# A decoder layer with eight experts on one core: new orders of the stages of each step, a router without casts, the last norm in nine batches, an expert's first rows fetched ahead of the next weights

## The reference

```python
x = ln(x + retention(x))          # 16 heads of 16; (q k^T * decay) v + 256 * q past_kv; group norm over the sequence
x = ln(x + cross_attention(x, ctx))  # 16 heads, causal softmax, Wo and bias
x = ln(x + experts(x))            # softmax router over 8 experts, the best two with weights that sum to 1
# an expert: gelu(x @ w_fc[e] + b_fc[e]) @ w_proj[e] + b_proj[e], hidden size 1024
```

## Time and profile before

| | |
|---|---|
| median of 3 runs | 1025.81 us (1024.01 to 1027.06) |
| the profiled execution, own time | 1028.0 us |
| its span in the profile | 1026.2 us |
| busy: TensorE, VectorE, ScalarE, GpSimd | 940.7 (92%), 674.0 (66%), 604.8 (59%), 386.6 (38%) |

### The profile page before, as it was taken

The page is one execution under the profiler, slowest core; times in us unless marked ns, Lnnn a source line. Parts: engine busy times, 40 slices in busy tenths (PEclk is TensorE's granted clock), DMA queues, the critical chain, the costliest instruction groups (busy, mean ns, idle before and its releaser), DMA issues.

```text
span 1026.2 us, 29954 instructions
## 1 busy us (share of the span) xinstructions
PE 940.7 (92%) x10845; PEld 827.9 (81%) x10845; DVE 674.0 (66%) x2054; ACT 604.8 (59%) x1521; POOL 386.6 (38%) x630
## 2 busy tenths in 40 slices
PE   5899999999999999999888998999999999999950
PEld 4788888887887887778777887999999999999950
DVE  3557877877777777787754674575565775575537
ACT  3456566565566665665546475566665675675534
POOL 0224544554455455554443422222232222233223
PEclk7899999999999999999989998999999999999985
DMA  8111131111111111113110434523425432523327
GB/s 271 46 33 53 49 126 64 44 64 55 52 44 54 54 59 48 43 49 110 38 43 27 104 65 121 133 43 55 130 44 139 116 63 42 143 42 46 47 41 317
DMA packets 57075, 79.92 MB, mean 78 GB/s; under 512 B 5696, under 2 KB 46016, under 8 KB 56832
## 3 DMA queue, kind: packets, MB, share of 16 engines
q1 hardware_dynamic: 41216, 58.50, 17.6%
q0 software_dynamic: 13536, 18.16, 10.5%
q10 hardware_dynamic: 2208, 1.73, 0.6%
HBM read 52.10 MB, written 29.71 MB: 80 GB/s over the span
## 4 chain that ended last, share of the span: by engine, by line
PE 53%; DVE 25%; ACT 8%; issue 7%; DMA 2%; POOL 2%; SPq 1%; another core or an unknown queue 0%; ACTq 0%; DVEq 0%; POOLq 0%
PE bank L799 14%; PE bank L813 9%; DVE row_max L1237 7%; PE bank L500 6%; PE bank L815 5%; DVE ret_p L1232 3%; PE bank L587 3%; PE bank L662 2%; PE bank L707 2%; PE bank L582 2%; ACT max_rows L1022 2%; ACT h_f L1131 2%; PE bank L615 2%; PE bank L636 2%; ACT h_parts L1125 2%
## 5 line engine op out<-in xcount | busy, mean ns | idle before, releaser
L799 PE MATMUL bank<-xs_hi,w_both 128*128 128x256 f32 x1152 | 243.9, 289 | 0.0
L1125 ACT ACTIVATE h_parts<-bank,bfc_s 128x256 fp32r<-128x256 f32 x288 | 140.0, 486 | 164.2 <-PE bank L799 158.6
L1679 POOL DMA_INDIRECT residual_sum<-y_w,meta_i x72 | 120.0, 1666 | 306.7 <-DVE y_w L1498 282.8
L1456 DVE TENSOR_TENSOR h_parts<-h_f,h_parts 128x256 fp32r<-128x256 f32 x288 | 121.5, 425 | 152.4 <-ACT h_f L1131 138.9
L813 PE MATMUL bank<-w_both,h_parts 128*128 128x512 f32 x544 | 200.5, 398 | 1.5 <-DVE h_parts L1456 1.5
L799 PEld LDWEIGHTS bank<-xs_hi,w_both 128*128 128x128 f32 x1152 | 193.0, 191 | 8.4 <-issue 2.3
L799 PE MATMUL bank<-xs_lo,w_both 128*128 128x256 f32 x576 | 163.7, 284 | 0.0
L815 PE MATMUL bank<-w_both,h_parts 128*128 128x256 f32 x544 | 153.3, 282 | 0.0
L1131 ACT ACTIVATE h_f<-bank,bfc_s 128x256 f32<-128x256 f32 x288 | 139.3, 484 | 4.4 <-DVE h_parts L1456 3.9
L813 PEld LDWEIGHTS bank<-w_both,h_parts 128*128 128x128 f32 x544 | 102.8, 189 | 20.4 <-DVE h_parts L1456 4.2
L799 PEld LDWEIGHTS bank<-xs_lo,w_both 128*128 128x128 f32 x576 | 110.5, 192 | 0.1
(11 more groups left out here) (185 smaller groups left out, 2161.5 us busy)
## 6 DMA issues: line engine op xcount, KB each, us to landing
rows<-sent_rows SPq DMA_DIRECT2D x37, 258.0 KB
xc_raw<-in_turned SPq DMA_DIRECT2D x32, 256.0 KB, 3.0
w_raw<-in_w_fc SPq DMA_DIRECT2D x8, 1024.0 KB
w_raw<-in_w_proj SPq DMA_DIRECT2D x8, 1024.0 KB
x_t<-in_x SPq DMA_DIRECT2D x32, 128.0 KB, 2.5
residual_sum<-x_row SPq DMA_DIRECT2D x32, 128.0 KB, 1.8
last_in<-residual_sum SPq DMA_DIRECT2D x8, 512.0 KB, 6.6
result<-last_out SPq DMA_DIRECT2D x8, 512.0 KB, 2.7
```

The costliest lines, as they stand in the source:

```text
L799: last = mm(ps_h(g, j), w[:, at:at + P], v[:, k, :], start=(n == 0), stop=(n == 3 * NCH - 1))
L1125: A(h_hi[j % 4][:, :], ps_h(g, j), ACT.Gelu_apprx_tanh, bias=bias)
L1456: V.tensor_tensor(h_lo[j % 4][:, :], h_f[j % 2][:, :], h_hi[j % 4][:, :].bitcast(f32), ALU.subtract).then_inc(s["h_split"], 1)
L1679: G.indirect_dma_start(total, bass.IndirectOffsetOnAxis(meta_i[:, half:half + 1], 0), y_w[:, half, :], None, compute_op=ALU.add)\
```

## The change

All engines get new lists for the steps. TensorE: max_turn(k-1) ends both kinds of step; prep_k and prep_kx stand right behind the scores; max_scores of the even step stands ahead of gn_mean. ScalarE: the four exponentials stand together, ahead of y_out. VectorE: row maxima ahead of ln1_stats in odd steps too; max_split(k-1) ends the even step and precedes pick in the odd. GpSimd: the even step holds shares of k-4 and of k-3, the odd none; in the odd step send stands ahead of gn_rstd. pick compares the integer index itself, put's sum writes integers itself. SP: expert e's first rows, then the weights of e+1 (for e from 1 to 6), then its other rows. The last norm has nine batches (256, seven times 512, 256 rows), and VectorE normalizes a row only in the last one.

For SP, the router and the last norm the diff stands with its minus lines:

```diff
+LAST = (2, 4, 4, 4, 4, 4, 4, 4, 2)
...
-NLAST = N_TOK // (4 * P)
-last_in = [sb(f"last_in{i}", [P, 4, C]) for i in range(NLAST)]
-last_out = [sb(f"last_out{i}", [P, 4, C]) for i in range(NLAST)]
+NLAST = len(LAST)
+last_in = [sb(f"last_in{i}", [P, n, C]) for i, n in enumerate(LAST)]
+last_out = [sb(f"last_out{i}", [P, n, C]) for i, n in enumerate(LAST)]
...
-GN, LN1, LN2, TOP, PUT, SHARE = 3, 3, 3, 4, 4, 4
+GN, LN1, LN2, TOP, PUT, SHARE = 3, 3, 3, 3, 3, 4
...
+def load_rows(e, at, g):
+    sp.wait_ge(s["rows_turned"], g + EVER)
+    sp.wait_ge(s["meta_ready"], g + EVER)
+    apart(sp)
+    sp.dma_start(rows[:, :, :],
+                 sent[ds(e, 1), ds(at, SLOT), :].rearrange("e (h p) c -> p (e h) c", p=P))\
+        .then_inc(s_rows, 16)
     apart(sp)
     for r in range(4):
         sp.wait_ge(s_sent[r], 32 * (B // 4))
-    with sp.Fori(0, n_slots) as j:
-        sp.wait_ge(s["rows_turned"], before + j + EVER)
-        sp.wait_ge(s["meta_ready"], before + j + EVER)
+    load_rows(e, 0, before)
+    if 0 < e < E - 1:
+        sp.wait_ge(s["raw_split"], e + 1)
         apart(sp)
-        sp.dma_start(rows[:, :, :],
-                     sent[ds(e, 1), ds(j * SLOT, SLOT), :].rearrange("e (h p) c -> p (e h) c", p=P))\
-            .then_inc(s_rows, 16)
-    if has_after:
-        sp.wait_ge(s["raw_split"], e + 2)
-        apart(sp)
-        load_weights(e + 2)
+        load_weights(e + 1)
+    with sp.If(n_slots > 1):
+        with sp.Fori(1, n_slots) as j:
+            load_rows(e, j * SLOT, before + j)
 experts(expert, slots)
...
-total_v = total[0:N_TOK, :].rearrange("(b p j) c -> b p j c", p=P, j=4)
-out_v = out.rearrange("b t c -> (b t) c").rearrange("(b p j) c -> b p j c", p=P, j=4)
+def rows_of(rows, b):
+    at = sum(LAST[:b]) * P
+    return rows[at:at + LAST[b] * P, :].rearrange("(p j) c -> p j c", p=P)
+out_rows = out.rearrange("b t c -> (b t) c")
-    sp.dma_start(last_in[b][:, :, :], total_v[b]).then_inc(s_last[b], 16)
+    sp.dma_start(last_in[b][:, :, :], rows_of(total, b)).then_inc(s_last[b], 16)
-    sp.wait_ge(s["last_act"], 3 * (b + 1))
-    sp.wait_ge(s["last_dve"], b + 1)
-    sp.dma_start(out_v[b], last_out[b][:, :, :]).then_inc(s["out_stored"], 16)
+    sp.wait_ge(s["last_act"], sum(LAST[:b + 1]) - (b == NLAST - 1))
+    if b == NLAST - 1:
+        sp.wait_ge(s["last_dve"], 1)
+    sp.dma_start(rows_of(out_rows, b), last_out[b][:, :, :]).then_inc(s["out_stored"], 16)
...
```

```diff
-for j in range(1, 4):
+for j in range(b == NLAST - 1, LAST[b]):
...
-ch.link(V.tensor_copy(top_f[:, :], top_i[:, 0:2]))
-                        top_f[:, :].unsqueeze(2).to_broadcast([P, 2, E]), ALU.is_equal))
+                        top_i[:, 0:2].unsqueeze(2).to_broadcast([P, 2, E]), ALU.is_equal))
-ch.link(V.reduce_sum(pos_f[:, :], place2[:, :, :], AX.X))
-ch.link(V.tensor_copy(pos[c.r][:, :], pos_f[:, :]))
+with nc.allow_low_precision(reason="places are whole numbers, summed in fp32 and written as integers"):
+    ch.link(V.reduce_sum(pos[c.r][:, :], place2[:, :, :], AX.X))
...
-    for j in range(4):
+    for j in range(LAST[b]):
-    for j in range(4):
+    for j in range(LAST[b]):
-    V.tensor_scalar(last_ve[:, b, :], last_mv[:, b, :, 1], EPS, None, ALU.add)\
+    V.tensor_scalar(last_ve[:, b, 0:LAST[b]], last_mv[:, b, 0:LAST[b], 1], EPS, None, ALU.add)\
-    V.scalar_tensor_tensor(out=last_nm[:, b, :], in0=last_mv[:, b, :, 0], scalar=-1.0,
-                           in1=last_rs[:, b, :], op0=ALU.mult, op1=ALU.mult)\
+    V.scalar_tensor_tensor(out=last_nm[:, b, 0:LAST[b]], in0=last_mv[:, b, 0:LAST[b], 0], scalar=-1.0,
+                           in1=last_rs[:, b, 0:LAST[b]], op0=ALU.mult, op1=ALU.mult)\
-    V.tensor_scalar(last_out[b][:, 0, :], last_in[b][:, 0, :], last_mv[:, b, 0, 0:1],
-                    last_rs[:, b, 0:1], ALU.subtract, ALU.mult).then_inc(s["last_dve"], 1)
+    if b == NLAST - 1:
+        V.tensor_scalar(last_out[b][:, 0, :], last_in[b][:, 0, :], last_mv[:, b, 0, 0:1],
+                        last_rs[:, b, 0:1], ALU.subtract, ALU.mult).then_inc(s["last_dve"], 1)
```

Of the step functions the new lists (lines that stay have no plus sign, though they may stand elsewhere in the list); the old ones stand in the code above. TensorE:

```diff
 def step(k):
     odd = k % 2
+    if not odd:
+        run(ret_scores, At(k))
+        run(att_back, At(k - 3))
+        run(x1_turn, At(k - 1))
+        pair_run(prep_kx, k // 2)
+        run(qx, At(k - 1))
+        run(att_proj, At(k - 3))
+        run(att_scores, At(k - 2))
+        run(ret_values, At(k))
+        run(rank, At(k - 4))
+        run(max_scores, At(k - 1))
+        run(gn_mean, At(k))
+        run(y_back, At(k))
+        run(x2_turn, At(k - 3))
+        run(att_values, At(k - 2))
+        run(logits, At(k - 3))
+        run(prep_v, At(k + 1))
+        run(o_turn, At(k - 2))
+        run(max_turn, At(k - 1))
     if odd:
+        run(ret_scores, At(k))
+        run(att_back, At(k - 3))
         pair_run(prep_k, (k + 1) // 2)
+        run(x1_turn, At(k - 1))
+        run(att_proj, At(k - 3))
+        run(qx, At(k - 1))
+        run(att_scores, At(k - 2))
+        run(ret_values, At(k))
+        run(rank, At(k - 4))
         pair_run(prep_q, (k + 1) // 2)
         run(gn_mean, At(k))
+        run(y_back, At(k))
+        run(max_scores, At(k - 1))
         run(x2_turn, At(k - 3))
+        run(att_values, At(k - 2))
+        run(logits, At(k - 3))
+        run(prep_v, At(k + 1))
+        if k < B - 1:
+            run(o_turn, At(k - 2))
             run(max_turn, At(k - 1))
```

ScalarE (its first lines, for k = -1, and its last, for weight splitting, are as before):

```diff
+    if not odd:
+        run(x1_T_out, At(k - 1))
+        if k >= 0:
+            pair_run(x_high, (k + 2) // 2, 0)
+        run(att_back_out, At(k - 3))
+        pair_run(kx_out, k // 2)
+        run(max_out, At(k - 2))
+        run(qx_out, At(k - 1))
+        for r in range(0, 2):
+            run(att_exp, At(k - 2), r)
+        for r in range(2, 4):
+            run(att_exp, At(k - 2), r)
+        run(y_out, At(k))
+        run(x2_T_out, At(k - 3))
+        run(o_out, At(k - 2))
+        run(v_out, At(k + 1))
+    if odd:
+        run(att_back_out, At(k - 3))
+        run(x2_again, At(k - 4))
         run(max_hi_out, At(k - 2))
+        run(x1_T_out, At(k - 1))
+        run(max_out, At(k - 2))
+        if k >= 0:
+            pair_run(x_high, (k + 2) // 2, 1)
         pair_run(k_out, (k + 1) // 2)
+        run(qx_out, At(k - 1))
+        for r in range(0, 2):
+            run(att_exp, At(k - 2), r)
+        for r in range(2, 4):
+            run(att_exp, At(k - 2), r)
+        if k == -1:
+            for dst, src, done in late_loads:
+                act.dma_start(dst, src).then_inc(s[done], 16)
+        run(y_out, At(k))
+        pair_run(q_out, (k + 1) // 2)
         run(x2_T_out, At(k - 3))
+        run(o_out, At(k - 2))
+        if k == -1:
+            w_high(3)
+        run(v_out, At(k + 1))
+        if k < B - 1:
+            run(x2_again, At(k - 3))
+            run(max_hi_out, At(k - 1))
     if k == 0:
         bits_out()
     if SPLIT <= k < SPLIT + HC // SPLITS:
```

VectorE:

```diff
 def step(k):
     odd = k % 2
+    if not odd:
+        for r in range(NT):
+            run(ret_decay, At(k), r)
+        pair_run(x_low, (k + 2) // 2, 0)
+        run(ln2_stats, At(k - 3))
+        run(put, At(k - 4))
+        run(ln2_norm, At(k - 3))
+        run(gn_moments, At(k))
+        for r in range(NT):
+            run(att_max, At(k - 1), r)
+        run(max_twice, At(k - 1))
+        run(gn_centre, At(k))
+        run(lg_out, At(k - 3))
+        run(ln1_stats, At(k))
+        run(att_norm, At(k - 2))
+        run(ln1_sum, At(k))
+        run(pick, At(k - 3))
+        run(ln1_norm, At(k))
+        run(max_split, At(k - 1))
     if odd:
+        for r in range(NT):
+            run(ret_decay, At(k), r)
+        run(ln2_stats, At(k - 3))
+        run(ln2_norm, At(k - 3))
         if k >= 0:
             pair_run(x_low, (k + 2) // 2, 1)
+        run(gn_moments, At(k))
+        run(put, At(k - 4))
+        run(gn_centre, At(k))
+        if k < B - 1:
+            for r in range(NT):
+                run(att_max, At(k - 1), r)
+            run(lg_out, At(k - 3))
         run(ln1_stats, At(k))
+        if k < B - 1:
             run(max_twice, At(k - 1))
             run(ln1_sum, At(k))
             run(att_norm, At(k - 2))
             run(ln1_norm, At(k))
             run(max_split, At(k - 1))
+            run(pick, At(k - 3))
     if SPLIT <= k < SPLIT + HC // SPLITS:
         for j in range(SPLITS):
             split_lo(0, 0, SPLITS * (k - SPLIT) + j)
```

GpSimd:

```diff
 def step(k):
+    if k % 2 == 0:
+        run(rstd, At(k - 3), l2rstd[:, :], l2var[:, :], "ln2_var", "ln2_rstd")
+        run(xb_, At(k))
         run(shares, At(k - 4))
+        run(gn_rstd, At(k))
+        run(rstd, At(k), l1rstd[:, :], l1var[:, :], "ln1_var", "ln1_rstd")
+        run(send, At(k - 4))
+        run(x1_bo_, At(k))
+        run(shares, At(k - 3))
+    else:
+        run(xb_, At(k))
+        run(rstd, At(k - 3), l2rstd[:, :], l2var[:, :], "ln2_var", "ln2_rstd")
+        run(send, At(k - 4))
+        run(gn_rstd, At(k))
+        run(rstd, At(k), l1rstd[:, :], l1var[:, :], "ln1_var", "ln1_rstd")
```

(76 more changed lines are left out.)

28 lines of the change are left out of this document (1 added, 27 removed).

## The result

| | before | after |
|---|---|---|
| median of four runs each, us | 1026.43 (1024.01 to 1029.60) | 1017.12 (1016.41 to 1018.19) |
| ratio, 95% interval | | 0.9905 (0.9878 to 0.9932) |
| profiled execution, its span | 1028.0, 1026.2 | 1016.69, 1014.6 |

What follows compares the result with a forecast made beforehand. TensorE was taken to bound attention and the experts, VectorE the last norm. Attention pairs -13.3, start -1, end of attention +3.5, experts -7, last norm -3 sum to -20.8, giving 1005 us, range 991 to 1019.

Steps and rivals of the forecast that it cites:

- The bound: Steady attention pairs: TensorE's order limits them; 31.1 us could fall to 29.2 without waits, 30.0 at worst.
- Fact (1): Both attention steps: max_turn last and prep products behind the scores remove the att_n and attT waits, about 0.8 us.
- Fact (2): Even steps: with exponentials ahead of y_out and max_scores ahead of gn_mean, TensorE gets a new wait of 0.5 us.
- Fact (3): Odd steps: sends ahead of gn_rstd delay the gn chain, so TensorE waits 0.6 us at max_turn, 0.65 with its drain.
- Fact (4): Step starts: VectorE begins ret_decay at 2.4 (even) and 2.65 (odd), costing att_scores 0 and 0.1 us of wait.
- C: Rival for attention: VectorE, not TensorE, ends each step; pair 32.9 us, total +18, 1044; chance 0.06.
- B: Rival for attention: GpSimd's scatters stretch, 1.3 us more a pair; total change about 0, 1025; chance 0.05.
- Start: First attention step: prep_kx(0) fills TensorE during VectorE's first ret_decay, -1 us (0 to 2 less).
- End of attention: Step 31: row maxima no longer cover the sends ahead of the gn chain, +3.5 us (0 to 4.5).
- Experts: Expert 1's first rows, loaded ahead of weights, remove TensorE's 5.1 us wait and 1.9 of half clock: -7.0 us.
- Last norm: Nine batches and less row normalizing on VectorE, which paces it: -3 us (-1.5 to -4).
- Rival D: Change does nothing that counts in attention (pair within 0.2), the rest stands: -7 to -9, 1018 us; chance 0.09.

Runs made afterwards that it cites:

- e1: The changed kernel with GpSimd's send in odd steps moved last, behind x1_bo, instead of ahead of gn_rstd: 992.38 us, ratio 0.9654.
- e10: The changed kernel with GpSimd's send in odd steps placed between gn_rstd and the rstd of ln1: 997.99 us, ratio 0.9718.
- e12: e1 with VectorE's part of splitting expert 0's weights moved into its wait behind ln2_stats, a step later: 990.47 us, ratio 0.9643.
- e11: e1 with ScalarE's y_out of even steps put back between the second and third exponential: 1021.85 us, ratio 0.9957.
- e5: The kernel before the change with the two router casts taken out and nothing else: 1018.27 us, ratio 0.9921.
- e9: e1 with the two router casts put back: 999.93 us, ratio 0.9746.
- e3: The changed kernel with the old step lists on TensorE, ScalarE, VectorE and GpSimd: 1009.74 us, ratio 0.9809.
- e8: The kernel before the change with step 0's prep_kx and its ScalarE copy moved earlier, the product right behind the retention scores: 1024.12 us, ratio 0.9987.
- e4: The changed kernel with GpSimd's send moved behind x1_bo in step 31 alone: 1010.75 us, ratio 0.9824.
- e6: The kernel before the change with SP's new expert order alone, an expert's first rows ahead of the next weights: 1018.39 us, ratio 0.9935.

## Why the prediction was wrong

Right direction, less than half the size. Step by step:

- **The bound.** I gave 29.2 for a pair in which TensorE never waits, "30.0 at worst, the busy time as it stands". e1, e10 and e12 all stop at 30.03, the busy time of before, though TensorE's rows show no idle time in e1's pair. But that pair holds about 0.5 of max_scores waiting for the exponentials, which its rows count as busy (below), so 30.03 is not a pair without waits. How much of the 0.9 of drains and short stops could still be had, no run shows.
- **Fact (1), right in direction.** The waits for att_n and attT are gone, the even step is 14.44 against 14.35.
- **Fact (2), right.** max_scores of an even step takes 1.62 from its first start to its last end, by the rows below, against 1.17 before: 0.45 of wait for the exponentials (0.5 forecast). e11 shows why they must stand ahead of y_out.

```profile
173.44 1.51 PE L647 MATMUL bank<-kxT,qx_own 32*128 32x128 f32 x31
...
174.79 0.27 PE L647 MATMUL bank<-kxT,qx_own 32*128 32x128 f32 x1
```

- **Fact (3), the step that failed: the term "the scatters start at 1.35".** The mechanism was right (e1: without it TensorE does not wait at max_turn), the size was not. The scatters start 2.03 after gn_mean, since one behind a wait takes 0.92 to start, not 0.2 to 0.35: x_pre at 5.78, not 5.1. That is 0.68. A further 0.26 is max_turn itself, which my count of the odd step left out between its wait and the next scores (6.85 to 7.11 after gn_mean). Together they make 16.0 into 16.93; over 13 pairs that is 12 of the 13.1 missed in steps 4 to 29. What the forecast called a wait of 0.65 costs 1.3 (e1). The trace of before already had the missing term: in its drain a scatter starts 0.98 after the last operation of put ends (548.87 + 0.17), as in the changed kernel's odd steps (190.54 to 191.53).

```profile
550.02 1.14 POOL L1669 DMA_INDIRECT sent_rows<-x_row,pos  x1 [2.53 <-DVEq L1342]
```

- **Fact (4), right:** ret_decay starts 2.51 and 2.70 into a step (2.4 and 2.65 forecast), and TensorE does not wait for it; C did not come.
- **Port and descriptors.** The scatters take 1.04 and 0.96 as before, beside row maxima (after) or not (e1): B did not come, and the row maxima left them alone.
- **Casts, wrong by itself.** I gave them no term. e5 measures 8 us in the old lists, e9 0.27 a pair in the new. The forecast held them only inside a pair's length. With the casts out of both, the new lists as written lost to the old ones (e3).
- **Start, undersized.** -1 against -5.5: the product covered the wait, but what counted was the half clock behind it (0.58 from 24 to 28 before): e8, with the product alone, has 3.3. The rest goes with a second such stretch, from 45 to 52 before; what ends that one is not shown.
- **End of attention, +3.5 against +3.5, for reasons that partly cancel.** The chain from gm to x_pre grew to 5.4 (508.29 to 513.70), 4.85 forecast; but the standstill of 4.54 us was followed by a half clock that I had not priced, so that the sends cost 7.9 up to the row maxima and 6.5 up to att_back (e4). Against that the trace of before had lost some 3 in its own drain (30.05; 26.9 in e5); with the old steps in e6 to e8 it is 1.0 to 2.5. So that measured and forecast 3.5 agree is in part luck.
- **Experts, right:** -7.0 against -7.9 in e6's trace and -6.7 in its times (-8.65 in the changed kernel's trace); weights issued later were late for nobody.
- **Last norm, too large:** -3 against about -1. VectorE's 2.0 a batch was right, but ScalarE starts its 29 unbroken rows 5.6 after the first statistics (991.19), where my 18.9 to its last row less their 14.5 left 4.4, that is 1.2 of the 2. The rest was not traced.
- **Rival D** (attention unchanged, rest as forecast, 1018, 0.09) is what the total looks like, by another way: attention gained 5.5 at its start, and gave 4.5 back.

## What to carry to other kernels

Before an operation is moved ahead of a short chain on an engine that works in order, ask what it waits for and who waits for the chain: two DMA issues of 2.3 us in front of a 1.4 us chain turned a good order (ratio 0.9654) into a middling one (0.9905), and a place a few lines lower cost nothing that the pairs show. Where the bounding engine would stand still for microseconds, count the half clock that may follow as well: at the end of attention 7.9 were lost to a chain that had grown by 3.75 (5.4 less 1.65). And price each small operation on an engine that is in the chain for a quarter of the span, even at 0.2 us: 64 of them made 8 (e5).
